# Linear attention: queries and keys normalised with channels on partitions, their means and deviations spread by transfers

## The reference, cut to what matters

```
q = hidden_states @ Wq                       # the same for k with Wk, v with Wv
beta = sigmoid(hidden_states @ Wb + bb)
gate = silu(hidden_states @ Wg)
q = silu(causal_dwconv(q, qconv_w, qconv_b)) # 4 taps along the tokens; k alike
q = layernorm(q, qn_w, qn_b)                 # over a head's 128 channels, each token; k alike
# per token: S = (1 - b) S + b v k^T ;  o = S q
out = (o * gate) @ Wo
```

## Time and profile before

| | us |
|---|---|
| median of 3 runs | 1081.63 (1079.57 to 1086.22) |
| the profiled execution | 1086.34 |
| its span on the core, first to last instruction | 1084.4 |
| PE busy, of the span | 1030.0 (95%) |
| DVE busy | 781.1 (72%) |
| ACT busy | 675.8 (62%) |
| POOL busy | 500.7 (46%) |

### The profile page before, as it was taken

One profiled execution on the slowest core, in us unless ns is written; L12 is line 12 of the kernel. 1 busy time (PEld: TensorE's weight loads), 2 busy tenths in 40 slices (PEclk: granted clock), 3 DMA queues, 4 the chain that ended last, 5 costly groups with the idle time before them and its releaser, 6 DMA issues. The chain is left out here.

```text
span 1084.4 us, 19328 instructions
## 1 busy us (share of the span) xinstructions
PE 1030.0 (95%) x6893; PEld 813.3 (75%) x6893; DVE 781.1 (72%) x1645; ACT 675.8 (62%) x1229; POOL 500.7 (46%) x441
## 2 busy tenths in 40 slices
PE   7899999999999988799999999999899999999997
PEld 5333333457788887699989998899789778888997
DVE  5779999736767846898999899999567455333843
ACT  4468888856554346888778878787456344333454
POOL 3332220114069551767686777677506000536644
PEclk9979999999999998899999999999999999999999
DMA  3533434204224301352123121311011123654200
GB/s 89 93 62 54 82 55 68 70 22 156 78 70 142 43 1 37 113 167 64 55 76 104 56 64 54 107 60 40 1 36 28 44 58 86 159 158 160 72 21 20
DMA packets 80634, 79.31 MB, mean 73 GB/s; under 512 B 29320, under 2 KB 67676, under 8 KB 80540
## 3 DMA queue, kind: packets, MB, share of 16 engines
q1 hardware_dynamic: 79872, 77.00, 27.1%
q10 hardware_dynamic: 668, 1.08, 0.5%
HBM read 65.51 MB, written 1.28 MB: 62 GB/s over the span
## 5 line engine op out<-in xcount | busy, mean ns | idle before, releaser
L706 ACT ACTIVATE attn_probs<-attn_rows_k 128x512 f32<-128x512 f32 x256 | 138.9, 595 | 33.5 <-PE attn_rows_k L554 30.6
L554 PE MATMUL attn_rows_k<-attn_q_stack,attn_k_stack 50*128 50x512 f32 x256 | 98.4, 465 | 0.0
L2899 DVE TENSOR_TENSOR late_mids<-late_mids,late_bank 128x512 f32<-128x512 f32 (+1 forms) x50 | 34.3, 687 | 78.2 <-PE late_bank L67 75.2
L810 DVE TENSOR_REDUCE attn_row_max<-s_sum 128x1 f32<-128x1024 f32 x62 | 75.6, 1220 | 15.8 <-PE attn_rows_q L538 7.4
L567 PE MATMUL attn_ctx<-attn_probs,attn_v 128*32 128x256 f32 x1024 | 85.4, 407 | 1.4
L810 DVE TENSOR_REDUCE attn_row_max<-attn_rows_q 128x1 f32<-128x1024 f32 x62 | 75.9, 1225 | 12.5 <-PE attn_rows_q L538 9.3
L65 PE MATMUL late_bank<-net_x_part_low,late_w_T 128*128 128x512 f32 (+1 forms) x192 | 77.9, 406 | 0.0
L66 PE MATMUL late_bank<-net_x_part_low,late_w_T 128*128 128x512 f32 (+1 forms) x192 | 76.1, 396 | 0.0
L67 PE MATMUL late_bank<-net_x_part_low,late_w_T 128*128 128x512 f32 (+1 forms) x192 | 76.1, 396 | 0.0
L1564 POOL TENSOR_TENSOR gold_mids<-gold_mids,s_later 128x512 f32<-128x512 f32 x32 | 52.9, 1691 | 45.0 <-DMA s_later<-gold_weights 45.0
L2804 ACT ACTIVATE late_mids<-late_bank 128x512 f32<-128x512 f32 (+1 forms) x50 | 29.9, 597 | 69.6 <-PE late_bank L67 69.6
(11 more groups left out here) (458 smaller groups left out, 3529.7 us busy)
## 6 DMA issues: line engine op xcount, KB each, us to landing
lin_mix<-decay_sums SPq DMA_DIRECT2D x16, 512.0 KB, 4.1
lin_q_dec<-decay_sums SPq DMA_DIRECT2D x16, 512.0 KB, 5.5
s_later<-gold_weights SPq DMA_DIRECT2D x16, 256.0 KB, 3.8
attn_k_stack<-s_part SPq DMA_DIRECT2D x30, 128.0 KB, 3.6
s_raw_ring<-in_L_ffn_Wg SPq DMA_DIRECT2D x12, 256.0 KB, 2.8
s_raw_ring<-in_L_ffn_Wu SPq DMA_DIRECT2D x12, 256.0 KB, 3.1
attn_q_stack<-s_part SPq DMA_DIRECT2D x32, 64.0 KB, 2.4
gold_raw_w_down<-in_L_ffn_Wd SPq DMA_DIRECT2D x1, 2048.0 KB, 12.3
```

Of the source, the lines that this page charges most:

```text
L554: pe.matmul(out, k_stack[rows, h % SLOTS, t * P:(t + 1) * P], q_stack[rows, h % SLOTS, :], start=True, stop=True).then_inc(scored_k, 1)
L706: act.activation(probs[:, (2 * k + odd) % PB, side * HALF:(side + 1) * HALF], ring_bank(("exped", 4 * k + n + 1)), ACT.Exp).then_inc(exped, 1)
L810: dve.tensor_reduce(row_max[h % 2][:, tile:tile + 1], ps_tile[tile_bank(n)][:, :], axis=AX, op=ALU.max)\
```

## The change

Queries and keys stay with channels on partitions for the normalisation itself. The turn to tokens on partitions (`rows_q`, `rows_k`) remains, for the statistics. The mean and the reciprocal deviation of each token, which lie as 128x8 with tokens on partitions, go by transfer to rows of 1024 floats in DRAM (`store_row`), one float at a time, and come back as one row read into all 128 partitions (`load_row`, 128x1024). VectorE then subtracts the mean row from the activated queries and multiplies with the deviation row, in place (`norm_q`, two instructions); GpSimd does so for the keys (`scale_k`). `q_T` and `k_T` are made from SBUF, and the turns back and their waits are gone. `silu` writes to tensors of its own, `acted`. `norm_q(n-1)` stands between the two convolutions of head n. On ScalarE `q_T(n-1)` stands ahead of `silu` of head n's queries and `k_T(n-1)` ahead of `silu` of its keys. The keys with tokens on partitions are normalised for seven chunks in place of eight (`norm_k`, `rows_k`, `decay_v`). SP gets eight transfers a head, at the head of its iteration. The rows lie in the space of w_o, so w_o is loaded in two halves after the last head's normalisation. (Declarations, the first heads' order, which follows the same pattern, and the two places that pass the new arguments are left out.)

```diff
@@ -1719,6 +1727,44 @@
                 sp.wait_ge(self.o_done, h - 1)
             sp.dma_start(self.q_dec[h % 2][:, :], self.decay_of(1, h)).then_inc(self.e_loaded[h % 2], 16)
+        def store_row(h, m, n, rows, done):
+            dram = self.norm_dram[2 * m + n].rearrange("(h t) -> h t", h=LH)
+            sp.dma_start(dram[h].rearrange("(c p) -> p c", p=P), rows, allow_slow_non_contiguous=True).then_inc(done[m], 16)
+        def store_mean(h, m):
+            sp.wait_ge((self.q_var, self.k_var)[m], h + 1)
+            store_row(h, m, 0, self.mean_var[m][:, :, 0], self.mean_stored)
+        def store_rstd(h, m):
+            sp.wait_ge((self.q_rstd, self.k_rstd)[m], h + 1)
+            store_row(h, m, 1, self.rstd[m][:, :], self.rstd_stored)
+        def load_row(h, m, n, rows, done):
+            dram = self.norm_dram[2 * m + n].rearrange("(h t) -> h t", h=LH)
+            sp.dma_start(rows[m], dram[h:h + 1, :].to_broadcast((P, T))).then_inc(done[m], 16)
+        def load_mean(h, m):
+            sp.wait_ge(self.mean_stored[m], 16 * (h + 1))
+            if h >= 1:
+                sp.wait_ge((self.q_centred, self.k_centred)[m], h)
+            load_row(h, m, 0, self.mean_rows, self.mean_loaded)
+        def load_rstd(h, m):
+            sp.wait_ge(self.rstd_stored[m], 16 * (h + 1))
+            if h >= 1:
+                sp.wait_ge((self.q_scaled, self.k_scaled)[m], h)
+            load_row(h, m, 1, self.rstd_rows, self.rstd_loaded)
+        def norm_rows(h):
+            store_mean(h, 0)
+            store_rstd(h, 0)
+            store_mean(h, 1)
+            load_mean(h, 0)
+            store_rstd(h, 1)
+            load_rstd(h, 0)
+            load_mean(h, 1)
+            load_rstd(h, 1)
         load_qk(1)
         sp.wait_ge(self.x_tail.low_done, 4)
         load_gate(0)
...
             if self.live(n - 1):
                 load_decay(n - 1)
+        sp.wait_ge(self.q_scaled, LH)
+        prefetch(sp, slice(0, LH // 2))
+        sp.wait_ge(self.k_scaled, LH)
+        prefetch(sp, slice(LH // 2, LH))
     def project_half(self, pe, m, half, out):
         cols = slice(half * HALF, (half + 1) * HALF)
...
@@ -1799,9 +1849,7 @@
         def rows_q(h):
             pe.wait_ge(self.q_acted, h + 1)
-            if h >= 1:
-                pe.wait_ge(self.q_T_done, h)
-            turn(pair[3], lambda c: self.conv[0][:, c * P:(c + 1) * P], self.q_rowed)
+            turn(pair[3], lambda c: self.acted[0][:, c * P:(c + 1) * P], self.q_rowed)
         def rows_k(h):
             pe.wait_ge(self.k_acted, h + 1)
@@ -1811,25 +1859,11 @@
                 pe.wait_ge(self.k_normed, 1)
             else:
                 pe.wait_ge(self.bias_ready, 1)
-            turn(pair[2], lambda c: self.conv[1][:, c * P:(c + 1) * P], self.k_rowed)
-        def turn_q(h):
-            pe.wait_ge(self.q_normed, h + 1)
-            if h + 1 < LH:
-                pe.wait_ge(self.q_conved, h + 2)
-            turn(pair[3], lambda c: self.normed[0][:, c, :], self.q_turned)
-        def turn_k(h):
-            pe.wait_ge(self.k_normed, h + 1)
-            if h + 1 < LH:
-                pe.wait_ge(self.k_conved, h + 2)
-            else:
-                pe.wait_ge(self.probs_done, h)
-            turn(pair[1], lambda c: self.normed[1][:, c, :], self.k_turned)
+            turn(pair[2], lambda c: self.acted[1][:, c * P:(c + 1) * P], self.k_rowed)
         def project_q(h):
             pe.wait_ge(self.q_split, h + 1)
-            pe.wait_ge(self.q_normed, h)
+            pe.wait_ge(self.q_var, h)
             project("q", pair[3], self.q_projected)
         def project_k(h):
...
@@ -1845,7 +1879,7 @@
             if h + 1 < LH:
                 pe.wait_ge(self.v_copied, h + 2)
             else:
-                pe.wait_ge(self.q_T_done, LH)
+                pe.wait_ge(self.q_var, LH)
             project("gate", pair[0] if h + 1 < LH else pair[3], self.g_projected)
         def project_v(j):
@@ -1869,6 +1903,10 @@
         def score(h):
             pe.wait_ge(self.q_T_done, h + 1)
             pe.wait_ge(self.k_T_done, h + 1)
+            if h + 1 < LH:
+                pe.wait_ge(self.k_conved, h + 2)
+            else:
+                pe.wait_ge(self.probs_done, h)
             for c in range(NT):
                 cols = slice(c * P, (c + 1) * P)
                 i = pe.matmul(pair[1][:, cols], self.k_T[:, cols], self.q_T[:, cols], start=True, stop=True)
@@ -1909,11 +1947,9 @@
         project_k(1)
         rows_k(0)
         project_q(1)
-        turn_q(0)
         for n in self.STEPS[2:LH + 1]:
             if live(n - 1):
                 rows_q(n - 1)
-            turn_k(n - 2)
             if live(n - 1):
                 rows_k(n - 1)
             project_gate(n - 2)
...
                 project_v(n)
-            if live(n - 1):
-                turn_q(n - 1)
             outputs(n - 2)
-        turn_k(LH - 1)
         key_values(LH - 1)
         score(LH - 1)
         project_gate(LH - 1)
...
@@ -1981,16 +2014,18 @@
             act.activation(self.e_last[:, :, :], self.ps_sum[1], ACT.Exp).then_inc(self.rows_ready, 1)
         def k_transposed(h):
-            act.wait_ge(self.k_turned, h + 1)
-            act.activation(self.k_T[:, :], self.pair[1][:, :], ACT.Identity, scale=self.norm_col[:, 2:3],
+            act.wait_ge(self.k_scaled, h + 1)
+            if h >= 1:
+                act.wait_ge(self.scored, h)
+            act.activation(self.k_T[:, :], self.acted[1][:, :], ACT.Identity, scale=self.norm_col[:, 2:3],
                            bias=self.norm_col[:, 3:4]).then_inc(self.k_T_done, 1)
         def q_transposed(h):
-            act.wait_ge(self.q_turned, h + 1)
+            act.wait_ge(self.q_scaled, h + 1)
             if h >= 1:
                 act.wait_ge(self.scored, h)
                 act.wait_ge(self.q_dec_done, h)
-            act.activation(self.q_T[:, :], self.pair[3][:, :], ACT.Identity, scale=self.norm_col[:, 0:1],
+            act.activation(self.q_T[:, :], self.acted[0][:, :], ACT.Identity, scale=self.norm_col[:, 0:1],
                            bias=self.norm_col[:, 1:2]).then_inc(self.q_T_done, 1)
         def silu_gate(h):
...
@@ -2006,26 +2041,27 @@
                 i = act.activation(mix[:, c, :], mix[:, c, :], ACT.Exp, bias=self.mix_bias[:, c, h:h + 1])
             i.then_inc(self.mix_exped, 1)
-        def tap(h, m, pair, projected, rowed, done):
+        def tap(h, m, pair, projected, done):
             act.wait_ge(projected, h + 1)
             if h >= 1:
-                act.wait_ge(rowed, h)
+                act.wait_ge((self.q_acted, self.k_acted)[m], h)
             act.activation(self.conv[m][:, :], self.pair[pair][:, :], ACT.Identity, scale=self.taps[:, m, h, TAPS - 1:TAPS],
                            bias=self.taps[:, m, h, TAPS:TAPS + 1]).then_inc(done, 1)
         def norm_k(h):
             act.wait_ge(self.shift_ready, h + 1)
             if h >= 1:
-                act.wait_ge(self.k_turned, h)
                 act.wait_ge(self.k_rows_done, h)
-            for c in range(NT):
-                i = act.activation(self.normed[1][:, c, :], self.tiled[2][:, c, :], ACT.Identity,
+            for c in range(NT - 1):
+                i = act.activation(self.k_normed_rows[:, c, :], self.tiled[2][:, c, :], ACT.Identity,
                                    scale=self.rstd[1][:, c:c + 1], bias=self.k_shift[:, c:c + 1])
             i.then_inc(self.k_normed, 1)
         def silu(h, m, conved, done):
             act.wait_ge(conved, h + 1)
-            act.activation(self.conv[m][:, :], self.conv[m][:, :], ACT.Silu).then_inc(done, 1)
+            if h >= 1:
+                act.wait_ge((self.q_T_done, self.k_T_done)[m], h)
+            act.activation(self.acted[m][:, :], self.conv[m][:, :], ACT.Silu).then_inc(done, 1)
         def copy_v(j):
             p, half = divmod(j, 2)
...
                 high_gate(n - 1)
+            if live(n - 1):
+                q_transposed(n - 1)
             if live(n):
                 silu(n, 0, self.q_conved, self.q_acted)
             if live(n - 1):
-                q_transposed(n - 1)
+                k_transposed(n - 1)
             if live(n):
                 silu(n, 1, self.k_conved, self.k_acted)
                 copy_v(n)
-        k_transposed(LH - 2)
         silu_gate(LH - 2)
         high_gate(LH - 1)
         exp_mix(LH - 1)
...
@@ -2169,19 +2206,19 @@
             dve.drain()
             if h >= 1:
                 dve.wait_ge(rstd, h)
+                dve.wait_ge(self.mean_stored[m], 16 * h)
             for c in range(NT):
                 dve.bn_aggr(self.mean_var[m][:, c, :], self.stats[m][:, c, :])
             dve.drain()
             dve.tensor_scalar(self.var_eps[m][:, :], self.mean_var[m][:, :, 1], EPS, None, ALU.add).then_inc(var, 1)
         def norm_q(h):
-            dve.wait_ge(self.q_rstd, h + 1)
-            if h >= 1:
-                dve.wait_ge(self.q_turned, h)
-            for c in range(NT):
```

(40 more changed lines are left out.)

63 lines of the change are left out of this document (37 added, 26 removed).

## The result

The changed kernel takes 1599.9 us (median of 4 runs, 1592.8 to 1603.9) against 1083.9 for the kernel before beside it: 1.479 times as long, 95% interval 1.473 to 1.484. The direction was forecast; of the 69 us expected there were 516. The profiled execution took 1592.8 us (span 1591.0, mean granted clock 0.821).

What follows compares the result with a forecast made beforehand. TensorE and VectorE were taken to hold each other at 22.04 us a head; chain 23.6 plus port 2.4 gives 26.0, so 15 periods add 59 us, 69 with the ends: 1151 us from 1081.6, range 1105 to 1195.

Steps and rivals of the forecast that it cites:

- Transfers: SP's stores and loads of statistic rows: the key mean reaches GpSimd after 8 to 9 us, so the round trip is narrowly covered.
- The upper bound: Landing of a single-float store: at most 4.5 us, taken from the convolution biases' transfer; 2.8 was assumed.
- Rival B: Rows come late through stores as slow as the biases, SP's queue fills: 28 us a head, 1183 us; chance 0.16.
- the late end: Landing of single-float stores, written below 512 B by read-modify-write: tends to the upper end of 1.9 to 4.5 us.
- The chain: From one project_q to the next through norm_q, q_T, silus, value copy and gate projection: 23.6 us a head.
- the upper side: Part of the range that holds TensorE's half-clock spells after idle time, costing up to 1.5 us each.
- Removing the turns: Two groups of transposes leave TensorE, 1.74 us a head; its demand falls to 20.0 us, VectorE's hardly.
- The port: VectorE's norm_q and GpSimd's scale_k take turns on SBUF: 2.7 us a head, 2.4 after drift; bounds 0 and 4.7.
- the ends: Uncovered round trips at the first and last head: 4 us for head 0 and 6 for head 15; bounds 3 and 15.
- VectorE's 21.1: VectorE's demand a head after the change, in us, with norm_q as two SBUF passes of 2.4 for 2.57 before.
- rival C: ScalarE's order has slack, so VectorE's demand of 21.1 us a head is the bound: 1068 us; chance 0.05.

Runs made afterwards that it cites:

- e10: Kernel before, with four stores a head of 1024 adjacent single floats added, which nothing waits for or reads; 1226.7 us.
- e14: Kernel before, with two added stores a head of 1024 adjacent single floats that nothing waits for; 1110.6 and 1152.0 us.
- e13: Kernel before, with four added stores a head of single floats 64 bytes apart that nothing waits for; 1084.6 us.
- e4: Changed kernel with loads reading other rows and the stored floats 64 bytes apart in DRAM; 1181.6 us.
- e7: Changed kernel, whole computation, with means and deviations turned on VectorE in 32x32 blocks, stored as 128-byte runs, two loads a head; 1181.8 us.
- e1: Changed kernel with another token order in DRAM, a partition's eight floats side by side; by packet count only the deviations' stores became 32-byte runs; 1233.6 us.
- e5: e3 with the second operand of both VectorE norm_q operations read from PSUM in every head but the last; 1141.5 us.
- e6: e3 with two buffers for activated rows, silus ahead of q_T and k_T on ScalarE, and two of four loads a head left; 1157.6 us.
- e3: Changed kernel without the stores and the waits for them; loads read decay rows once the statistics are ready; 1162.9 us.
- e2: Changed kernel with its stores and waits kept, but each load reads a decay row written before the first head; 1572.5 us.

## Why the prediction was right or wrong

**Transfers: the step that failed.** "I take 1.0 to issue (half as many) and 2.8 to land, between 1.9 and 4.5", and "So the round trip is covered by decay_q and what precedes it, narrowly." In the head shown the stores issued in 0.4 to 0.6 us, but over all heads the last of the four took 3.6 in the median. They were confirmed one after the other, 13.9, 16.0, 23.3 and 27.5 us after their issue (25.5 in the median for the last), and the loads, put at 4.1, took 16.4. The upper bound, 4.5 from the bias row, was no bound: that row is a load, in which the floats are gathered from DRAM, and the stores write them to DRAM as neighbours. It was the nearest row by shape and the wrong one by direction. (It wasn't even the slower of its kind: the issue of 2.46 in the earlier trace rows is the query bias's, and that load landed in 5.7.) And all four stores were priced one by one, as a latency; the head shown, e10 and e14 show that they share a limited rate and that four in a head fill the queue. Rival B had the mechanism (rows late, queue full) with 28 us a head for 53.3, because it used the same row. The Trainium skill, DMA: Bandwidth & Descriptors, section "Specifications", says that below 512 B the engine reads, modifies and writes. I turned that into "the late end". By the runs the size alone doesn't decide it: single floats 64 bytes apart cost nothing where nobody waits for them (e13), 1.0 us a head where the head does (e4), and 128-byte runs land in 1.4 us (e7); many single writes close together are what costs. The same page's "Rules for kernel authors" says that a strided last dimension becomes one descriptor per element and should be rearranged; e1's packet counts agree, and e7 is that advice.

**Order and chain.** The chain was put at 23.6 us. e5, without stores and port stalls, has 25.3. I put the missing 1.7 down to TensorE's half clock, which I had left to the upper side; no run separates it. In one head of e5 it waits 2.4 us for silu, then the eight turns of the keys take 1.97 us for 1.04 before, and the gate projection 4.4 (570.12 to 574.53) for 2.9: 2.4 us more together. That this is a chain through single buffers was only half right: with two buffers and e6's other changes the head gives back 0.8 us, and another in-order queue holds it.

**The port.** The mechanism stands (e3, e5), though the changed kernel itself shows none of it (1.23 us for both operations). It was mis-sized: 2.4 us a head taken, 1.2 measured.

**The sum without the failed step.** 26.0 us a head was forecast, e3 has 26.5; and its span is 77 us longer than before where 69 were forecast. That this is so near is partly luck, since four errors cancel. Over 15 heads the port was put 18 us too high (1.2 each) and the chain with its clock 26 too low (1.7 each); the ends, put at 10, cost nothing beyond the 15 heads; and the heads before take 21.4 us on average, not the 22.04 of the one that I measured, another 10 too low. -18 + 26 - 10 + 10 is the 8 us by which e3 is longer. (With the stores the start isn't free: the first head's state comes 27.5 us later than before.)

**VectorE and TensorE demand.** Removing the turns gave nothing, as forecast. No run isolates it, but in e3 TensorE is busy 249.6 of 300 us (clock 0.89) and waits for silu, so its work isn't the bound. VectorE's 21.1, on which rival C rests, left out a wait: `shift_k`, which had `norm_q` ahead of it before, now waits for `power`, 19.3 us in 11 heads of e3.

## What to carry to other kernels

Before values go to DRAM to be spread over partitions, look at the destination of each element: if elements written singly are neighbours there, from different partitions or from one, make runs of 128 bytes first (one turn in 32x32 blocks on VectorE) or leave gaps (32 bytes were enough here). Price such stores for the queue that they share, not only for their own landing: loads beside and behind them are late too. And take a bound only from a row that moves data in the same direction; where there is none, the range must say that it isn't bounded.

## What was not expected of the hardware

- Stores of 1024 single floats that fill 4 KB of DRAM were confirmed one after the other, four of them in 41.8 us, and 512 KB loads of unrelated data beside them landed in 16.3 us for 4.9 (e2, e3). 64 bytes apart, the same number cost the kernel before nothing (320.7 us for 15 heads against 320.8).
- Eight successive floats of one partition side by side, written singly, from a strided source, are slower (32.5 us a head) than neighbours from different partitions (29.1).
- Which unit (DRAM piece, bank, transfer engine) serialises these writes is open. The runs show that two writes in 64 bytes do no harm, eight some and sixteen much. A wider spacing also makes the region larger (64 KB a store at 64 bytes), and no run here varied one engine or the region alone.
